# Second attention of a four-stage transformer block: two head pairs per slot instead of one

## What is computed

```python
x = x + _L0_xattn_ref(_layernorm(x, axis=-1), ctx_1024, ...)
x = x + _L0_ffn_ref(_layernorm(x, axis=-1), ...)
x = x + _L1_xattn_ref(_layernorm(x, axis=-1), ctx_1024, ...)   # this stage
x = x + _L1_ffn_ref(_layernorm(x, axis=-1), ...)

def _L1_xattn_ref(x, context, ln_gamma, ln_beta, w_q, w_kv, w_out, b_out, gate):
    xn = _layernorm(x, ln_gamma, ln_beta)
    q = (xn @ w_q).reshape(B, SQ, NUM_HEADS, DIM_HEAD)
    k, v = jnp.split(context @ w_kv, 2, axis=-1)
    ...
    scores = jnp.einsum('bqhd,bkhd->bhqk', q * SCALE, k)
    attn = jax.nn.softmax(scores, axis=-1)
    out = jnp.einsum('bhqk,bkhd->bqhd', attn, v).reshape(B, SQ, INNER)
    return (out @ w_out + b_out) * jnp.tanh(gate[0])
```

## Time and profile before

| engine | busy over the span, us | share of the span |
|---|---|---|
| PE | 1709.7 | 94% |
| PEld | 1461.9 | 80% |
| DVE | 1313.3 | 72% |
| ACT | 1144.5 | 63% |
| POOL | 825.5 | 45% |

### The profile page before, as it was taken

One profiled execution on the slowest core, in us unless ns is written; L12 is line 12 of the kernel. 1 busy time (PEld: TensorE's weight loads), 2 busy tenths in 40 slices (PEclk: granted clock), 3 DMA queues, 4 the chain that ended last, 5 costly groups with the idle time before them and its releaser, 6 DMA issues.

```text
span 1823.8 us, 41775 instructions
## 1 busy us (share of the span) xinstructions
PE 1709.7 (94%) x16112; PEld 1461.9 (80%) x16112; DVE 1313.3 (72%) x2808; ACT 1144.5 (63%) x2880; POOL 825.5 (45%) x1300
## 2 busy tenths in 40 slices
PE   5799999999999999999999889999999999997778
PEld 4567676679899999999999767888888888876655
DVE  4789989551707888888888486777777777668447
ACT  1377677523347777777777477777777777764330
POOL 2235433110103333333331487888888887764200
PEclk7799999999999999999999999999999999999789
DMA  7755556246876666666676722222222222111378
GB/s 187 207 134 121 128 132 120 80 155 237 295 257 211 243 244 243 243 243 243 244 241 221 243 76 65 93 65 70 63 95 66 69 63 89 53 56 48 99 209 296
DMA packets 131815, 284.99 MB, mean 156 GB/s; under 512 B 13921, under 2 KB 74593, under 8 KB 118945
## 3 DMA queue, kind: packets, MB, share of 16 engines
q1 hardware_dynamic: 110880, 169.81, 30.9%
q0 software_dynamic: 20736, 112.51, 18.1%
HBM read 199.95 MB, written 82.05 MB: 155 GB/s over the span
## 4 chain that ended last, share of the span: by engine, by line
PE 75%; DVE 10%; DMA 5%; POOL 5%; issue 4%; ACT 0%; SPq 0%; DVEq 0%; POOLq 0%; ACTq 0%
PE ps L1250 12%; PE ps L1236 12%; PE ps L1998 5%; PE ps L373 5%; PE ps L219 5%; PE ps L2029 4%; PE ps L1984 4%; PE ps L2018 4%; PE ps L379 4%; PE ps L464 3%; PE ps L440 3%; DVE NM L592 2%; POOL P L209 2%; PE ps L540 2%; PE ps L452 2%
## 5 line engine op out<-in xcount | busy, mean ns | idle before, releaser
L196 ACT ACTIVATE P<-ps,NM 128x256 f32<-128x256 f32 x512 | 236.3, 481 | 127.5 <-DVE NM L185 127.5
L209 POOL TENSOR_TENSOR P<-P,RS 128x1024 f32<-128x1024 f32 x128 | 242.9, 1903 | 73.9 <-DVE RS L203 73.5
L1236 PE MATMUL ps<-XRP,W1P 128*128 128x256 f32 x1872 | 227.1, 281 | 3.3 <-DVE W1P L1319 3.3
L1236 PEld LDWEIGHTS ps<-XRP,W1P 128*128 128x128 f32 x1872 | 220.4, 190 | 3.6 <-DVE W1P L1319 3.6
L1250 PE MATMUL ps<-W2P,HP 128*128 128x256 f32 x1872 | 221.9, 277 | 0.0
L1250 PEld LDWEIGHTS ps<-W2P,HP 128*128 128x128 f32 x1872 | 218.5, 188 | 0.0
L592 DVE TENSOR_REDUCE NM<-ps 128x2 f32<-128x512 f32 x256 | 164.4, 684 | 38.2 <-PE ps L440 36.5
L690 ACT ACTIVATE PT<-ps 128x512 f32<-128x512 f32 x256 | 139.2, 597 | 69.7 <-PE ps L452 67.5
L185 DVE TENSOR_REDUCE NM<-ps 128x2 f32<-128x512 f32 x256 | 164.6, 685 | 5.8 <-PE ps L1984 4.2
L1170 POOL DMA_INDIRECT WE<-in_we,WIX x39 | 44.3, 1135 | 269.2 <-DVE W1P L1319 208.8
L1279 ACT ACTIVATE HF<-ps,WE 128x256 f32<-128x256 f32 x312 | 129.0, 465 | 43.3 <-PE ps L1236 43.3
(11 more groups left out here) (236 smaller groups left out, 3740.2 us busy)
## 6 DMA issues: line engine op xcount, KB each, us to landing
KS<-k_scratch SPq DMA_DIRECT2D x64, 256.0 KB, 2.9
V<-v_scratch SPq DMA_DIRECT2D x16, 1024.0 KB, 6.1
k_scratch<-KVM SPq DMA_DIRECT2D x52, 256.0 KB, 3.9
QS<-q_scratch SPq DMA_DIRECT2D x96, 128.0 KB, 4.4
v_scratch<-KVM SPq DMA_DIRECT2D x40, 256.0 KB, 3.0
ys_scratch<-YS SPq DMA_DIRECT2D x39, 256.0 KB, 8.0
ctx_scratch<-CHL SPq DMA_DIRECT2D x32, 256.0 KB, 2.7
CHR<-ctx_scratch SPq DMA_DIRECT2D x16, 512.0 KB, 4.8
```

What stands on the lines that cost most here:

```text
L196: i = e.activation(self.P[u % 4][:, c, :], PS[SB[n % 3]][:, y * 256:y * 256 + 256], ACT.Exp, bias=self.NM[:, u % 4, c:c + 1], accum_out=se ...
L209: e.tensor_tensor(p, p, self.RS[:, u % 4, :].unsqueeze(2).to_broadcast([128, 4, 256]), ALU.mult).then_inc(self.s_pn, 1)
L1236: m = e.matmul(PS[p][:, hh * 256:hh * 256 + 256], W1P[i % 2][wi][:, cc * 1024 + hc * 128:cc * 1024 + hc * 128 + 128], XRP[i % 2][xi][:, cc ...
```

## The change

A slot now takes two pairs (a double slot); 64 double slots take the place of 128 slots. The instructions are the same in kind and number on every engine; their order, their PSUM banks and their waits change.

- PE in double slot i: scores of pairs 2i and 2i+1 (four score banks), turns of pair 2i-2, a quarter of a result, turns of pair 2i-1, in two of four slots a `turn_x`, queries for slot i+2, values of pairs 2i-3 and 2i-2.
- Queries and result share one bank (`WB`); the turned input shares the bank of the values, which now has two halves. A group of queries waits for the DVE to have added the result before it, and a result waits until the queries before it are taken; values in a slot with `turn_x` wait for `scale_x`.
- DVE: split, maxima, split, maxima, `result_add`, first reciprocals, `scale_x` and two adds (slots 0 and 1 of a batch), statistics (`stats_out` in slot 1, `stats_x` in slot 2), second reciprocals, `queries_low`.
- ACT: exponentials, turn copies, exponentials, turn copies, queries, keys.
- POOL: both `norm_pool` of the slot's own pairs, `keys_low`, `input_low` (slots 0 and 1), and then in slot 1 a `newton` and two gathers, in slot 2 the other `newton` and two gathers.

```diff
     SB, TB, OB = (0, 1, 2), (3, 4), 5
+    SB1, TB1, OB1, WB = (0, 1, 2, 3), (4, 5), PS[7], PS[6]
...
+    def results_in(i):
+        if i < 5:
+            return ()
+        if i <= SLOTS1:
+            return (i - 5,)
+        return {SLOTS1 + 1: (60, 61), SLOTS1 + 2: (62, 63)}.get(i, ())
+    def queries_in(i):
+        return tuple(d for d in ((1, 2) if i == 0 else (i + 2,)) if d < SLOTS1)
+    def values_in(i):
+        return tuple(u for u in (2 * i - 3, 2 * i - 2) if 0 <= u < U)
...
-        for i in range(SLOTS):
-            g, r = i // 8, i % 8
-            if i < U:
-                scores(i)
-            if r == 0 and is_batch(g):
-                queries(g, 1)
-            elif r == 1 and is_batch(g - 2) and g < 17:
-                result(g - 2, 1, 0)
...
-            if 0 <= i - 3 < U:
-                a1.turn_pe(e, w, i - 3)
...
-            if 0 <= i - 4 < U:
-                values(i - 4, now)
+        for i in range(SLOTS1 + TAIL1):
+            g, n = i // 4, i % 4
+            split = min(max(0, 2 * i - 3), U)
+            for u in (2 * i, 2 * i + 1):
+                if u < U:
+                    scores(u)
+            if i == 0:
+                queries(1, 0)
+            if 0 <= 2 * i - 2 < U:
+                a1.turn_pe(e, w, 2 * i - 2)
+            for x in results_in(i):
+                result(x, results_before(i), min(queries_before(i), 64))
+            if 0 <= 2 * i - 1 < U:
+                a1.turn_pe(e, w, 2 * i - 1)
+            if n < 2 and is_batch(g + 1):
+                turn_x(g + 1, n, split)
+                turned += 1
+            for d in queries_in(i)[-1:]:
+                queries(d, results_before(i + 1))
+            for u in values_in(i):
+                values(u, split, turned)
...
+            if n < 2 and is_batch(g + 2):
+                add(g + 2, 2 * n)
+                add(g + 2, 2 * n + 1)
+            if n == 1 and is_batch(g - 2) and g < 17:
+                stats_out(g - 2)
+            elif n == 2 and is_batch(g + 2):
                 stats_x(g + 2)
...
+            if i < SLOTS1:
+                a1.recip_dve(e, w, 2 * i + 1)
...
+        for i in range(SLOTS1 + TAIL1):
+            g, n = i // 4, i % 4
+            if i < SLOTS1:
+                a1.norm_pool(e, w, 2 * i)
+                a1.norm_pool(e, w, 2 * i + 1)
+            if i + 2 < SLOTS1:
+                keys_low(i + 2)
+            if n < 2 and is_batch(g + 1):
+                input_low(g + 1, n)
+            if n == 1:
+                if is_batch(g - 2) and g < 17:
+                    newton(e, w, stat1["o", g - 2], 2 * (g - 2), 2, RSTD)
                 if is_batch(g + 3):
                     gather(g + 3, 0)
...
                     gather(g + 3, 1)
+            elif n == 2:
                 if is_batch(g + 2):
                     newton(e, w, stat1["a", g + 2], 2 * (g + 2), 2, RSTD)
+                if is_batch(g + 3):
+                    gather(g + 3, 2)
+                    gather(g + 3, 3)
```

More of the change, by code:

```diff
@@ L1432, in build, with scores_read, results_before, queries_before @@
     s_om, s_bo = sem("outmm1"), sem("bias1")
-    QB, RB = PS[7], PS[6]
     s_qb, s_rb = a1.s_m
-    STEP0 = U + 1
-    SLOTS = STEP0 + 20
+    SLOTS1 = U // 2
+    TAIL1 = 21
     stat1 = {("a", 0): len(stat0), ("a", 1): len(stat0) + 1}
-    for i in range(SLOTS):
-        for r, kind, b in ((6, "a", i // 8 + 2), (7, "o", i // 8 - 2)):
-            if i % 8 == r and 0 <= b < 16 and (kind, b) != ("o", 15):
+    for i in range(SLOTS1 + TAIL1):
+        for r, kind, b in ((1, "o", i // 4 - 2), (2, "a", i // 4 + 2)):
+            if i % 4 == r and 0 <= b < 16 and (kind, b) != ("o", 15):
                 stat1[kind, b] = len(stat0) + len(stat1)
     stat1["o", 15] = len(stat0) + len(stat1)
-    def scores_read(b, n):
-        return 2 * (8 * (b - 1) + 2 * n + 1) + 2
+    def scores_read(d):
+        return 4 * (d - 4) + 4
+    def results_in(i):
[8 more added lines that the diff above has]
+        return tuple(u for u in (2 * i - 3, 2 * i - 2) if 0 <= u < U)
+    def results_before(i):
+        return sum(len(results_in(x)) for x in range(i))
+    def queries_before(i):
+        return 1 + sum(len(queries_in(x)) for x in range(i))
+    def result_part(x):
+        b, k = x // 4, x % 4
+        c0 = 256 * (k % 2) if b == 15 else 0
+        return b, k % 2, k // 2, WB[:, c0:c0 + 256]
+    def input_part(b):
+        return (OB1 if b else PS[TB1[1]])[:, 0:256]
+    def value_half(u):
+        c0 = 256 * (1 - u % 2)
+        return c0, c0 + 256
     def half(z, cc):
@@ L1988, in scores, with values @@
                             m.then_inc(a1.s_sc, 1)
-        def values(u, turned):
+        def values(u, split, turned):
             b, p = u // 8, u % 8
+            c0, c1 = value_half(u)
             w.wait_ge(d_vl[b % 2], 16 * (b // 2 + 1))
             w.wait_ge(a1.s_tv, 2 * u + 2)
-            w.wait_ge(a1.s_ot, 2 * u)
+            w.wait_ge(a1.s_ot, 2 * split)
             w.wait_ge(s_xh, turned)
@@ L2025, in result @@
             w.wait_ge(a1.s_ot, 2 * (8 * b + 4 * half + 4))
-            w.wait_ge(s_rb, 2 * b + lt)
+            w.wait_ge(s_rb, added)
+            w.wait_ge(s_qb, asked)
             for cc in range(4 * half, 4 * half + 4):
-                for x, (oi, wi) in enumerate(PAIRS):
-                    e.matmul(RB[:, 0:256], OT1[b % 2][oi][:, cc, lt * 128:lt * 128 + 128], W1O[wi][:, cc, :],
-                             start=(cc == 0 and x == 0), stop=False)
+                for n, (oi, wi) in enumerate(PAIRS):
+                    m = e.matmul(M, OT1[b % 2][oi][:, cc, lt * 128:lt * 128 + 128], W1O[wi][:, cc, :],
+                                 start=(cc == 4 * half and n == 0), stop=(not half and cc == 3 and n == 2))
             if half:
                 for j in range(2):
-                    m = e.matmul(RB[:, 0:256], EYE[:, :], BOS[j][:, :], start=False, stop=(j == 1))
-                m.then_inc(s_om, 1)
+                    m = e.matmul(M, EYE[:, :], BOS[j][:, :], start=False, stop=(j == 1))
+            m.then_inc(s_om, 1)
         w.wait_ge(s_ye, NTF)
@@ new lines, in dve_l1 @@
+            if 0 <= 2 * i - 5 < U:
+                values_split(2 * i - 5, done)
+            if i < SLOTS1:
+                a1.max_dve(e, w, 2 * i)
+            if 0 <= 2 * i - 4 < U and i <= SLOTS1 + 1:
+                values_split(2 * i - 4, done)
+            if i < SLOTS1:
+                a1.max_dve(e, w, 2 * i + 1)
+            if i == 0:
+                norms(1, 0)
+                norms(1, 1)
+                queries_low(1)
+            for x in results_in(i):
+                result_add(x, results_before(i + 1))
@@ L2209, in dve_l1 @@
+            if i < SLOTS1:
+                a1.recip_dve(e, w, 2 * i + 1)
+            for d in queries_in(i)[-1:]:
+                queries_low(d)
+            if i == SLOTS1 + 3:
+                stats_out(15)
+            if i >= SLOTS1:
+                dve_step(e, w, i - SLOTS1 - 1)
         dve_tail(e, w)
     def act_l1(e, w):
-        def queries_high(b, n):
-            w.wait_ge(s_qm1, 4 * b + n + 1)
-            w.wait_ge(a1.s_sc, scores_read(b, n))
-            e.activation(flat(Q1[0][:, 2 * n:2 * n + 2, :]), QB[:, :], ACT.Copy).then_inc(s_qh, 1)
@@ L2245, in act_l1 @@
         w.wait_ge(s_ye, NTF)
-        keys_high(0, 0)
-        keys_high(0, 1)
+        keys_high(0)
+        keys_high(1)
         w.wait_ge(d_w0_w1, 96)
```

260 lines of the change are left out of this document (101 added, 159 removed).

## The result

The changed kernel takes 1859.0 us (median of four runs, 1854.9 to 1864.3) against 1820.3 us before in the same comparison: a ratio of 1.021 (95% interval 1.0188 to 1.0232), 38.7 us or 2.1% slower. Its profiled execution has a span of 1853.1 us, 29.3 more than the 1823.8 before; that execution itself took 1854.9.

The account below looks back on a forecast made before the run. PE bound the old kernel; the new order would be bound by a loop through DVE, POOL and PE. Span 1823.8 + 15 (waits for POOL, less gains) + 13 (half clock) = 1852, runs 3.3 shorter: 1849 us; range 1792 to 1868.

Parts of the forecast that it names:

- Rival 1: PE's clock does not fall behind its waits for POOL: 1836 us, 1828 to 1842; chance 0.25.
- rival 2: PE alone decides, no waits for POOL, 35 us gained at the passages: 1785 us, up to 1795; chance 0.20.
- rival 3: A draw: DVE reaches slot 1's second reciprocals in time, period 36.4 us: 1813 to 1826 us; chance 0.15.
- half clock per batch: PE in slot 0, behind the 2.6 us wait: 1.2 us longer at half clock, 13 us over 11 batches.
- start: first scores, batches 0 and 1: Batches 0 and 1 wait for queries and weights in either order: 0, between -5 and +5 us.
- The loop: Batches 2 to 12: 8.8 us in slot 1, 22.6 on POOL, 7.1 on PE make 38.5 us, 2.0 more than before.
- The clock's row: Earlier trace's nearest row: 3.33 us idle on PE, then granted clock 0.50; taken as evidence for the clock's fall.
- The passages: PE's longer steps between kinds of work, made once per two pairs: 0.55 us each time saved, 2.4 us a batch.
- ACT's copies: Turn copies on ACT delay PE 0.2 us in every second slot, at most 6 us; taken as 0.
- a first batch over 5 us longer: Sign against the prediction: a first batch more than 5 us longer than before would show it wrong.
- The end: Last steps after the attention: same number of groups remains after the last scores, 0, between -5 and +5 us.
- From span to runs: Step from profiled span to run time: runs taken as 3.3 us shorter, 1852 to about 1849 us.

Follow-up runs that it names:

- e3_busy_wait: Changed kernel plus 14 matmuls nobody reads, filling PE's wait in slot 0 of batches 3 to 13: 1849.0 us, ratio 1.017 to the kernel before.
- e8_spread_adds: Changed kernel with POOL's extras and DVE's statistics spread over slots, ACT's turn copies between exponential halves, DVE's adds before first reciprocals: 1787.8 us, ratio 0.9828.
- e1_gathers: Changed kernel with POOL's gathers 0 and 1 moved from slot 1 to 0, gathers 2 and 3 from slot 2 to 3: 1817.5 us, ratio 0.999.
- e2_stats: Changed kernel with DVE's statistics of the result moved from slot 1 to slot 0: 1840.1 us, ratio 1.0127 to the kernel before.
- d1_extra_slot2: Changed kernel with one POOL key split done twice in slot 2 of ten batches: 1875.2 us, one run.
- d2_extra_slot0: Changed kernel with one POOL key split done twice in slot 0 of ten batches: 1859.9 us, one run.
- e4_act: Changed kernel with ACT's copies of the first turns moved between the two halves of the exponentials: 1854.8 us, ratio 1.0185 to the kernel before.

## Why the prediction was right, and where it was off

The forecast was 1849 us, from a profiled span of 1852; measured were 1859.0 and 1853.1. Rival 1 (no fall of the clock) is out by the row at 0.50, rival 2 (PE alone decides) by the 22 waits, rival 3 (DVE early enough) by POOL's wait of 2.46 us.

| step | predicted | measured |
|---|---|---|
| product of slot 1 starts after | 8.8 us | 9.14 |
| POOL without a gap | 22.6 | 22.94 |
| PE's rest of slot 0, full clock | 7.1 | 7.08 (e3_busy_wait) |
| half clock per batch | 1.2 | 1.56 |
| PE's waits in slots 3 and 0 | 1.8, 2.6 | 1.40, 2.50 |
| batch if PE alone decides | 34.1 | 34.28 and less (e8_spread_adds) |
| batches 2 to 12 | +35 | +42.2 |
| start: first scores, batches 0 and 1 | 0 | -4.1 + 7.4 |
| last three batches and end | -7 + 0 | -1.4 (13, 14), -14.8 (from batch 15 on) |

**The loop is shown**, not only argued: taking the gathers out of it (e1_gathers), making DVE's part shorter (e2_stats) and POOL's longer (d1_extra_slot2) move the batch, and the same dose outside (d2_extra_slot0) does not. The mis-sized terms are small but have one sign: 0.34 us each on DVE and POOL and 0.36 for the clock. DVE's is `scale_x`, which starts 5.63 us after the scores instead of 5.3; POOL's is the two chains, 3.85 and 3.82 us to the next instruction instead of 3.63. Batch 2 had no wait in its slot 0 (36.7 us from slot 0 to slot 0), batch 11 no half clock (39.2) and batch 12 two (42.9).

**The clock's row.** The prediction says that no idle time of 2.6 us occurs in this stage before. That holds for its middle, not for its first batch: PE stands there for 3.27 us ahead of 1045.44 and for 2.36 ahead of 1049.46, and in the stretch 1044.40 to 1054.50 the granted clock is 0.50. These rows lie nearer than the earlier trace rows and speak for the same choice.

**The passages** were worth about what was said, 2.25 us a batch instead of 2.4. With POOL, DVE and ACT out of the way (in e8_spread_adds no wait of PE is listed from 1100 to 1580), a batch falls from 36.53 to 34.28 us; the earlier trace rows carried that estimate.

**ACT's copies** were taken at nothing. They cost 0.34 us in a double slot (e4_act), hidden in the eleven batches but not in batch 14, where 34.1 was expected and 34.89 came; the measured 10.4 us of waits lie above the bound of 6. At the start there is no result group between the two turns to cover the copies: PE waits 3.01, 1.59 and 1.59 us for them in slots 1 to 3, and batch 0 is 5.5 us longer than before. The prediction had named a first batch over 5 us longer as a sign against it; its term of 0 for the start was wrong by this and by the wait for the weights. The first scores came 4.1 us earlier; they lie between 1035.4 and 1042.6 us in the traces of the new order, so a difference of 4.1 is within their scatter.

**The end** was the largest error, and it hid the others. I had said that the same number of groups remains after the last scores. But the last result moved closer. The first scores of the last batch and the last bias matmuls of the result (timeline of PE; kernel before, then the changed one):

```profile
1591.51 0.98 PE L1984 MATMUL ps<-K,Q 64*128 64x256 f32 x12
...
1656.35 0.40 PE L2033 MATMUL ps<-BOS,EYE 128*128 128x256 f32 x2
```

```profile
1635.56 1.70 PE L2020 MATMUL ps<-K,Q 64*128 64x256 f32 x24
...
1684.16 0.40 PE L2075 MATMUL ps<-BOS,EYE 128*128 128x256 f32 x2
```

That distance fell from 64.8 to 48.6 us, and the end of the span came 14.8 us closer to those scores as well (217.5 instead of 232.3; 214.6 to 223.3 in the twelve traces of the new order). The new order puts the last four quarters into two slots (`results_in`); that stood in the diff, and I did not look. No run changes it alone, so that the end follows from it is argued, not shown. The sum of the span came out at +29 against +28 because this, the start and the loop nearly cancel: that the forecast of the span lies within 1 us is luck, while its direction and its mechanism are not.

**From span to runs.** I subtracted 3.3 us; the profiled run of the changed kernel took 1.8 us more than its span, and the other three were 4 to 9 us above that one. Every execution listed took 1.8 to 3.5 us more than its own span; the 3.3 us set the span of one execution against the median of others, and executions of the kernel before lie between 1813.8 and 1829.2 us in the comparisons here. Most of the miss of 10 us in the median is here.

**The two rules weighed.** The Trainium skill, "Perfetto Trace Analysis", Identifying the Most-Contended Engine, says to optimise the engine with the highest occupancy first, but to judge TensorE's headroom by other measures than its matmul busy time, the busy share of the weight loads among them. The prediction left the second half out: PE's 99.5 us in the earlier trace rows point to PE, but the weight loads' 81.0 lie below POOL's 85.6. Here the engine at 86% bound, through the order of its work, and PE's pace decided only once that order was mended (e8_spread_adds). The Trainium skill, "TensorE: Matmul & The Clock Gate", Part 1 (HAM oscillation), says that pauses bring the half rate. The rows agree for nine of eleven batches of the changed kernel, while in e2_stats an equal idle time did so only in six.
